# Decayed linear attention and a top-2 expert layer on one core: the normalisations' shifts go to VectorE, and VectorE, ScalarE and PE take their work of a chunk in new orders

## What is computed

```python
def _layernorm(x, axis=-1, eps=1e-05):
    m = jnp.mean(x, axis=axis, keepdims=True)
    v = jnp.var(x, axis=axis, keepdims=True)
    return (x - m) / jnp.sqrt(v + eps)

x = x + _L0_attn_ref(_layernorm(x), W_write, W_read, decay, log_alpha)
x = x + _L0_ffn_ref(_layernorm(x), gate_w, w1, b1, w2, b2)
```

```python
def scan_fn(W, chunk):
    rk_c, wk_c, v_c = chunk
    inter = jnp.einsum('bij,bcj->bci', W, rk_c) * g_p[:, :, None]
    S = jnp.einsum('bcd,bkd->bck', rk_c, wk_c)
    intra = jnp.einsum('bck,bkd->bcd', S * M, v_c)
    W_new = g_C[:, None, None] * W + jnp.einsum('bci,bcj->bij', v_c * g_w[:, :, None], wk_c)
    return (W_new, inter + intra)
...
return out + (reads @ W_read.T).astype(out.dtype)
```

## Time and profile before

| | us |
|---|---|
| median of 3 runs | 571.51 |
| lowest and highest of them | 568.94, 571.64 |
| span of the profiled execution, first to last instruction | 576.6 |
| of that, steps 3 to 15 of DVE | 130.7 (22.3 to 153.0) |
| PE busy in the span | 534.6 (93%) |
| DVE busy | 457.3 (79%) |
| ACT busy | 332.8 (58%) |
| POOL busy | 244.5 (42%) |

### The profile page before, as it was taken

How to read it: one execution, slowest core, us unless ns; L and a number is a source line. 1 busy time by engine, 2 the same in 40 slices (tenths; PEclk the granted TensorE clock), 3 DMA queues, 4 the chain that set the end, 5 groups by cost and what they waited for, 6 DMA issues and landing times.

```text
span 576.6 us, 17660 instructions
## 1 busy us (share of the span) xinstructions
PE 534.6 (93%) x5246; PEld 418.7 (73%) x5246; DVE 457.3 (79%) x1408; ACT 332.8 (58%) x841; POOL 244.5 (42%) x275
## 2 busy tenths in 40 slices
PE   7799889899988888999999999999999999999991
PEld 7677777777776656777777777777777777777770
DVE  5889999999976789777887877777777887877771
ACT  5899989888744633444545444544454545444540
POOL 2426778888846532432333222333332333222333
PEclk8999999999998979999999999999999999999996
DMA  5577767667334353444444344444444433444432
GB/s 162 199 221 224 254 205 214 188 216 215 122 96 123 113 179 58 78 71 68 67 65 62 63 70 75 78 75 75 70 71 67 68 62 62 65 69 76 76 48 27
DMA packets 85097, 63.34 MB, mean 110 GB/s; under 512 B 54224, under 2 KB 77392, under 8 KB 85008
## 3 DMA queue, kind: packets, MB, share of 16 engines
q1 hardware_dynamic: 71328, 43.94, 31.0%
q0 software_dynamic: 13392, 18.27, 17.1%
q10 hardware_dynamic: 288, 0.00, 0.0%
HBM read 37.56 MB, written 24.62 MB: 108 GB/s over the span
## 4 chain that ended last, share of the span: by engine, by line
PE 63%; DVE 13%; POOL 8%; issue 8%; ACT 3%; SPq 1%; DMA 1%; another core or an unknown queue 0%; ACTq 0%; DVEq 0%; POOLq 0%
PE psum L1518 29%; PE psum L1533 20%; PE psum L1535 10%; POOL sent_rows L501 4%; DVE weights L779 2%; POOL tiny L491 2%; POOL tiny L488 1%; DVE arena L915 1%; SPq L429 1%; PE psum L1338 1%; DVE tiny L858 1%; DMA arena<-in_x 1%; DVE tiny L881 1%; DVE arena L1146 1%; DVE arena L851 1%
## 5 line engine op out<-in xcount | busy, mean ns | idle before, releaser
L1518 PE MATMUL psum<-arena,weights 128*128 128x256 f16 (+1 forms) x2208 | 281.4, 250 | 4.3 <-issue 4.3
L1518 PEld LDWEIGHTS psum<-arena,weights 128*128 x2208 | 188.8, 99 | 83.1 <-issue 6.6
L737 ACT ACTIVATE arena<-psum,b_cur 128x256 f32<-128x256 f32 (+1 forms) x368 | 131.7, 423 | 159.9 <-PE psum L1518 120.4
L532 POOL DMA_INDIRECT out<-arena,tile_in x71 | 115.0, 1620 | 251.6 <-DVE arena L1161 150.3
L1533 PE MATMUL psum<-weights,arena 128*128 x568 | 215.7, 381 | 2.1 <-DVE arena L1148 2.1
L1535 PE MATMUL psum<-weights,arena 128*128 x568 | 155.4, 274 | 0.0
L1148 DVE TENSOR_TENSOR arena<-arena 128x512 f16<-128x512 f32 x142 | 99.6, 701 | 4.9
L501 POOL DMA_INDIRECT sent_rows<-arena,tiny x64 | 65.3, 1021 | 27.3 <-issue 16.6
L1146 DVE CAST arena<-arena 128x512 f16<-128x512 f32 x142 | 61.8, 435 | 6.1 <-ACT arena L737 5.8
L1533 PEld LDWEIGHTS psum<-weights,arena 128*128 128x128 f16 x568 | 55.8, 98 | 8.7 <-issue 2.6
L1535 PEld LDWEIGHTS psum<-weights,arena 128*128 128x128 f16 x568 | 55.8, 98 | 4.8
(11 more groups left out here) (172 smaller groups left out, 641.8 us busy)
## 6 DMA issues: line engine op xcount, KB each, us to landing
weights<-in_experts SPq DMA_DIRECT2D x32, 512.0 KB
arena<-sent_rows SPq DMA_DIRECT2D x100, 64.0 KB
arena<-in_b SPq DMA_DIRECT2D x46, 128.0 KB
arena<-in_x SPq DMA_DIRECT2D x16, 256.0 KB, 3.7
out<-arena SPq DMA_DIRECT2D x16, 256.0 KB, 4.1
arena<-sent_rows SPq DMA_DIRECT2D x84, 32.0 KB
sent_rows<-pad SPq DMA_DIRECT2D x7, 265.0 KB
tile_in<-sent_rows SPq DMA_DIRECT2D x71, 4.5 KB
```

The source lines that it names most:

```text
L532: pool.indirect_dma_start(out=out, out_offset=bass.IndirectOffsetOnAxis(ap=at_u, axis=0), in_=yout[:, u % 4], in_offset=None, compute_op=A ...
L737: last = a.activation(act[:, g % 2, m * n:(m + 1) * n], ps_h[:, g % 2, m * n:(m + 1) * n], ACT.Gelu_apprx_tanh, scale=1.0 / WSCALE, bias=b ...
L1518: last = pe.matmul(ps_h[:, f % 2, mm * n:(mm + 1) * n], w1_of(e_of[i], k, lo, per * (f - GROUP[i]) + mm), turned[:, i % 2, part, k, 0:n], ...
```

## The change

- **Shifts.** POOL no longer makes them. It keeps the sum with epsilon and the power. DVE makes each shift with one instruction, in two new functions: `chunk_shift(n)` for the first normalisation and `residual_shift(n - 3)` for the second. Each waits for POOL's power. `moments1` now has two buffers.
- **Order on DVE.** `carry` goes behind `chunk_low`, `choose` behind `residual`. The last two remainders of a step stand together at its end, and only a third one stands in the middle.
- **Order on ACT.** `normed_transposed` goes from behind `chunk_values` to the front of `chunk_high`; `chunk_residual` goes from before `chunk_keys` to behind `chunk_values`; the last high part goes behind `chunk_normalise`.
- **Order on PE.** `turn_normed` goes before `project`, and `score_experts` before `states`.
- **Pieces.** Step 2 takes two pieces and step 7 takes two; so steps 3 to 6 have three, 7 to 15 two.

```diff
-PIECES = (0, 0, 1, 3, 3, 3, 3, 3, 2, 2, 2, 2, 2, 2, 2, 2)
+PIECES = (0, 0, 2, 3, 3, 3, 3, 2, 2, 2, 2, 2, 2, 2, 2, 2)
...
-        moments1 = by_batch(small(B * 2))
+        moments1 = [by_batch(small(B * 2)) for _ in range(2)]
...
-                        pool.tensor_scalar(ve, moments[:, :, 1], EPS, None, ALU.add)
-                        pool.tensor_scalar(shift, moments[:, :, 0], -1.0, None, ALU.mult).then_inc(S[mid], 1)
+                        reached(pool, end, m - 1)
+                        pool.tensor_scalar(ve, moments[:, :, 1], EPS, None, ALU.add).then_inc(S[mid], 1)
                         reached(pool, mid, m)
                         pool.tensor_tensor(rs, ve, minus_half[:].to_broadcast([P, B]), ALU.pow).then_inc(S[end], 1)
-                        reached(pool, end, m)
-                        pool.tensor_tensor(shift, shift, rs, ALU.mult).then_inc(S[last], 1)
...
+            def chunk_shift(n):
+
+                reached(v, "rs1_done", n)
+                v.scalar_tensor_tensor(out=shift1[n % 2], in0=moments1[n % 2][:, :, 0], scalar=-1.0, in1=rs1[n % 2],
+                                       op0=ALU.mult, op1=ALU.mult).then_inc(S["shift1_done"], 1)
...
+            def residual_shift(m):
+
+                reached(v, "rs2_done", m)
+                v.scalar_tensor_tensor(out=shift2, in0=moments2[:, :, 0], scalar=-1.0, in1=rs2, op0=ALU.mult,
+                                       op1=ALU.mult).then_inc(S["shift2_done"], 1)
...
-                for j in splits(n)[0:1]:
+                if active(n, 5):
+                    choose(n - 5)
+                for j in splits(n)[:-2]:
                     split_low(j)
                 if active(n, 3):
                     residual_stats(n - 3)
+                if active(n, 0):
+                    chunk_shift(n)
...
+                if active(n, 3):
+                    residual_shift(n - 3)
...
-                for j in splits(n)[1:]:
+                for j in splits(n)[-2:]:
                     split_low(j)
```

More of the change, by code:

```diff
@@ L210, in build @@
         small_at = [0]
-        tiny = sb("tiny", [P, 188])
+        tiny = sb("tiny", [P, 192])
         def small(w, dt=F32):
@@ L477, in step @@
                 par = n % 2
-                for lag, moments, ve, rs, shift, got, mid, end, last, used, ago in (
-                        (0, moments1, ve1, rs1[par], shift1[par], "moments1_done", "ve1_done", "rs1_done",
-                         "shift1_done", "res_done", 1),
-                        (3, moments2, ve2, rs2, shift2, "moments2_done", "ve2_done", "rs2_done", "shift2_done",
-                         "xm_done", 0)):
+                for lag, moments, ve, rs, got, mid, end, used, ago in (
+                        (0, moments1[par], ve1, rs1[par], "moments1_done", "ve1_done", "rs1_done", "res_done", 1),
+                        (3, moments2, ve2, rs2, "moments2_done", "ve2_done", "rs2_done", "xm_done", 0)):
                     if active(n, lag):
@@ L682, in step @@
                     last_column(n - 1)
+                if active(n, 4):
+                    normed_transposed(n - 4)
                 if active(n, 1):
@@ L686, in step @@
                     split_high(j)
-                if active(n, 1):
-                    chunk_residual(n - 1)
                 if active(n, 5):
@@ L692, in step @@
                     chunk_keys(n - 1)
-                for j in splits(n)[1:2] if len(splits(n)) > 2 else ():
+                for j in splits(n)[1:-1]:
                     split_high(j)
@@ L696, in step @@
                     chunk_values(n - 2)
-                if active(n, 4):
-                    normed_transposed(n - 4)
-                for j in splits(n)[2:] if len(splits(n)) > 2 else splits(n)[1:]:
-                    split_high(j)
+                if active(n, 1):
+                    chunk_residual(n - 1)
                 if active(n, 0):
                     chunk_normalise(n)
+                for j in splits(n)[1:][-1:]:
+                    split_high(j)
                 if n == NCH + 1:
@@ L718, in _ @@
             chunk_keys(1)
-            split_high(0)
+            for j in splits(2):
+                split_high(j)
             reads_high(0)
@@ L937, in step @@
                     largest(n - 5)
-                if active(n, 3):
-                    carry(n - 3)
                 if active(n, 0):
                     moments(n)
-                if active(n, 5):
-                    choose(n - 5)
                 if active(n, 1):
@@ L949, in step @@
                                   zcol[:]).then_inc(S["xlo_done"], 1)
+                if active(n, 3):
+                    carry(n - 3)
                 if active(n, 1):
@@ L1239, in _ @@
             moments(1)
+            chunk_shift(0)
             first_normalise(0)
@@ L1242, in _ @@
             first_residual(0)
+            chunk_shift(1)
             first_normalise(1)
@@ L1252, in _ @@
             chunk_queries(0)
+            chunk_shift(2)
             mask_decay()
@@ L1268, in _ @@
             split(0)
+            residual_shift(NCH - 1)
             place(m)
@@ L1448, in step @@
                     turn_chunk(n - 1)
+                if active(n, 4):
+                    turn_normed(n - 4)
                 if active(n, 3):
                     project(n - 3)
-                if active(n, 4):
-                    turn_normed(n - 4)
                 if active(n, 2):
@@ L1458, in step @@
                     rank(n - 5)
+                if active(n, 4):
+                    score_experts(n - 4)
                 if 2 <= n <= NCH:
                     states(n - 2)
-                if active(n, 4):
-                    score_experts(n - 4)
                 if active(n, 2):
```

6 lines of the change are left out of this document (3 added, 3 removed).

## The result

The changed kernel takes 579.09 us (median of 4 runs, 578.40 to 584.92) where the kernel before takes 570.23 (median of 4, 567.43 to 571.64) beside it: 1.018 times as long, interval 1.012 to 1.024. The forecast was 569.2 with a range from 565.0 to 575.5, so it is slower by about 9 us where a small gain was forecast. The profiled execution of the changed kernel took 578.4 us; its span is 576.6, the same as that of the profile before. In that profile stage two, whose code is the same, took 402.0 us (174.6 to the end) and here 395.9 (180.7 to the end), so stage one has to be compared by its own stretches.

The account below looks back on a forecast made before the run. The prediction took POOL to bound the two-piece steps (10.3 us). Steps 2 to 15 give 0.9 us and the stretch behind step 15 1.4, together 2.3: 571.5 - 2.3 = 569.2 us, range 565.0 to 575.5.

Parts of the forecast that it names:

- POOL is the bound of the two-piece steps: Steps 8 to 15, before the change: POOL runs without a break, 10.3 us a step, 1.95 of it from two stretched operations.
- POOL falls to 7.3 us: POOL in a two-piece step: 10.3 less 1.1 for the shifts and up to 1.95 for the collisions with remainders.
- The DMAs under the pair of remainders cost 0.3 us, hidden: POOL's DMAs at the step's end: 1.35 us instead of 1.08 seen, 0.3 taken, hidden by 2 us in hand.
- Rival 3: POOL can't issue DMAs during both remainders, starting 2.35 us later; two-piece steps 10.7 us, 578 in all; chance 0.03.
- Shifts cost DVE 0.08 us each and don't wait: DVE's two new shifts, 0.2 us a step with new waits; DVE's own pace 9.5 us (two-piece) and 10.6 (three-piece).
- The longer loop sets 9.7 and 10.9 us: Round through DVE, PE, ACT and back to `chunk_low`, lengthened by the new orders: two-piece steps 9.7 us, three-piece 10.9.
- rival 1: The loop doesn't bind and DVE's own pace holds, 9.5 us in two-piece steps; 566.0 us in all; chance 0.22.
- ACT's* late `chunk_residual` is wanted two steps later.: ACT's order: the moved residual's result is needed only two steps later; no cost was put on it.
- The sum: Steps 2 to 15: 1.1 + 19.6 + 21.8 + 87.3 = 129.8 us against 130.7, 0.9 less.
- The term of 1.4 us behind step 15: After step 15: 1.4 us gained, from ACT entering step 16 without its 1.22 us wait and 0.2 for sooner logits.
- Rival 2: ACT waits for `turn_normed` in front of `chunk_high`, lengthening the loop 0.5 us in all 13 steps; 576.9 us; chance 0.15.
- Rival 4: The loop at its upper end, 9.9 and 11.3 us a step, eats POOL's gain; 571.9 us; chance 0.15.

Follow-up runs that it names:

- before_again: The kernel before, unchanged, run again for a second profile on the chip of the later runs: 571.35 us (one run).
- third_x: The changed kernel with three buffers for x instead of two, so SP's load and store wait for older residuals: 579.02 us, 1.0004 of the kernel before.
- residual_back_again: The changed kernel with chunk_residual back in its old place on ACT, ahead of exponential and chunk_keys, second measurement: 579.05 us, 1.0016 of the kernel before.

## Why the prediction was wrong, point by point

- **POOL is the bound of the two-piece steps.** Right for the execution that was read, wrong as a size. In before_again POOL is as unbroken, but its walk takes 9.7 us, since L488 takes 0.68 us under the remainder and not 1.23. That is 2.6 us over steps 8 to 14 which the forecast counted as there to be gained.
- **POOL falls to 7.3 us.** Right, and more: 6.6 us busy in the changed kernel, 6.2 in third_x. No small operation of POOL is stretched in steps 8 to 15, and it waits for DVE's moments each step (12.3 us in 9 places). Timeline of POOL after, which answers the earlier trace rows:

```profile
83.56 1.41 POOL L482 DMA_INDIRECT sent_rows<-arena,tiny  x1 [1.52 <-DVE tiny L832]
85.27 0.96 POOL L482 DMA_INDIRECT sent_rows<-arena,tiny  x1 [0.30 <-issue]
...
88.79 0.24 POOL L472 TENSOR_SCALAR tiny<-tiny 128x2 f32<-128x2 f32 x1
89.12 0.72 POOL L474 TENSOR_TENSOR tiny<-tiny,minus_half 128x2 f32<-128x2 f32 x1
91.14 0.22 POOL L472 TENSOR_SCALAR tiny<-tiny 128x2 f32<-128x2 f32 x1 [1.30 <-DVE tiny L854]
```

- **The DMAs under the pair of remainders cost 0.3 us, hidden.** Right in the usual case: the first takes 1.41 us, 0.45 more than the 0.96 of the others. But the row of 1.35 us was read wrongly. Its issue started at 71.32 and ended at 72.67, 0.95 us behind the end of the first of the two remainders (70.50 + 1.22 = 71.72); it was held up whole by that one and got in before the second. By the Trainium skill (SBUF — State Buffer, section "SBUF: two separate sides"), GpSimd can't write descriptors while DVE holds the shared ports. The rows of 1.35, 1.41 and 2.54 us agree, and so do L488 and L493. Rival 3 came in single steps of the later kernels, as steps of 10.5 or 10.6 us (it said 10.7). It isn't what the changed kernel lost: none of its DMAs in steps 8 to 15 took over 1.98 us.
- **Shifts cost DVE 0.08 us each and don't wait.** Right in the changed kernel and third_x; behind a DMA issue of 2.54 us, in residual_back_again, the first one waits 0.83 us. DVE's own pace was forecast as 9.5 us; third_x shows 9.6.
- **The longer loop sets 9.7 and 10.9 us.** The steps came out near it, by another cause in one of two cases. In third_x the two-piece steps are DVE's own 9.6 us, so there rival 1 was right and the loop doesn't bind. Of its three-piece steps (forecast 10.9) the loop binds step 5, 11.4 us: PE waits 1.5 us for `weigh_scores`, ACT 0.66 for `reads`, DVE 0.70 for `chunk_high`. In step 6, 10.7 us, DVE waits for nobody, so this is again its own pace, forecast as 10.6.
- **"*ACT's* late `chunk_residual` is wanted two steps later."** This is the step that failed. It is true of the DVE operation that reads the result, and I looked at no other reader of `res_done`. But the instruction also frees the buffer of x, and SP's load of the next chunk waits for that in the same step, with the store and all pieces queued behind it. The order rows of ACT in the change, and SP's rows in a trace, would have shown it. Price: 137.1 - 129.5 = 7.6 us in steps 3 to 15, the changed kernel's profile against third_x's (6.8 of them in steps 8 to 15, at full clock), and 1.1 to 1.9% of the time. On the chip where both ran, third_x takes all of it back by changing what the load and the store wait for, and nothing else.
- **The sum** of the steps was near once the queue is free: 129.5 us in third_x for steps 3 to 15 against 128.7, and 8.0 instead of 7.4 in step 2, for which 1.1 more was forecast. The term of 1.4 us behind step 15 came to nothing: from the end of step 15 to stage two are 21.6 us before, 21.6 after and 21.9 in third_x. So third_x only equals the kernel before (1.0004), and the forecast of -2.3 us lies just outside its interval (-1.5 to +1.9 us of 579).
- **Rivals.** Rival 2 (ACT waits for `turn_normed`) would have given a time 2 us from the measured, 576.9, but did not happen: L557 has no wait for PE in the timeline of ACT. Rival 3's 578 was near the measured time too, by luck: no issue is held through the whole pair in steps 8 to 15 of this profile. The measured slowdown is a mechanism that no rival had. Rival 4, nothing left, names what third_x measures, but not by its reason, a loop at its upper end.

## What to carry to other kernels

When an instruction is moved later, list everybody who waits for its semaphore, not only who reads its result: an instruction that frees a buffer releases a load, and everything queued behind that load on the issuing engine comes later too. An engine that only issues DMAs has no busy column; its waits have to be asked for by themselves, before and after. And a bound that rests on two engines' phase (a 1.23 us collision that is 0.68 us in the next execution) should be read from more than one execution before a gain is put on its removal. When a stretched duration is to tell what holds an instruction, look at where it ends, not only at how long it is: 1.35 us looked short of a block and ended one issue behind the instruction that held it.

## What the runs showed that was not expected

- One SP queue makes a loop, of 10.93 us in the round shown, out of 3.80 us of ACT, 2.28 us of issuing and 4.85 us of transfer, in steps where no engine is busy for more than 9.5 on average. The Trainium skill (DMA: Bandwidth & Descriptors, section "Anatomy of one DMA — SWDGE (gpsimd) path") says that a DMA's semaphore wait happens on the issuing sequencer before dispatch; SP's store and pieces, which leave only behind the load of x, agree.
- A DMA issue of POOL that starts under a pair of DVE remainders takes 1.41 us or 2.54 us, starting at the same place, 0.75 us into the pair. The second makes a 9.6 us step 10.6.
- PE's granted clock falls to 1.2 GHz for 3.4 or 6.8 us inside a stage in which PE is busy for nine tenths, in one step behind an idle time of 1.33 us and in another, behind the same idle time, not. One of 3.4 us makes a 9.6 us step 11.2, and the single runs of a kernel spread over 8 us and more, the slower ones at lower mean clocks.
- The same kernel settles into two-piece steps of 10.3 us in one execution and 9.7 in another at the same clock, and a POOL operation of 0.2 us falls otherwise there against a DVE operation of 1.22.
